# Moving the first expert's PSUM eviction from VectorE to ScalarE in a fused recurrent-attention and mixture-of-experts layer

## The reference

```
r  = sigmoid(xn @ Wr.T);  k = xn @ Wk.T;  v = xn @ Wv.T
scale  = exp(position * log(sigmoid(decay)))
state  = cumsum(k * v / max(scale, 1e-10), over tokens) * scale
s      = rmsnorm(r * state) @ Wo.T

scores = xn @ gate_w.T                        # 8 experts
onehot = one_hot(argmax(scores))
moe    = xn + sum over e of onehot[e] * (xn @ expert_w[e].T)
out    = x + s * silu(moe)
```

## Time and profile before

| | |
|---|---|
| time, median of 3 runs | 1269.22 us (1264.96 to 1271.9) |
| the profiled execution, its own time | 1270.49 us |
| its span on the slowest core (core 1) | 1268.9 us (other cores from 1261.4 us) |
| TensorE busy, matmuls | 910.5 us, 72% |
| VectorE busy | 691.3 us, 54% |
| ScalarE busy | 453.0 us, 36% |
| mean granted TensorE clock, core 1 | 0.911 of full speed |

### The profile page before, as it was taken

One profiled execution on the slowest core, in us unless ns is written; L12 is line 12 of the kernel. 1 busy time (PEld: TensorE's weight loads), 2 busy tenths in 40 slices (PEclk: granted clock), 3 DMA queues, 4 the chain that ended last, 5 costly groups with the idle time before them and its releaser, 6 DMA issues.

```text
span 1268.9 us, 17472 instructions; the slowest of 8 cores (1261.4 to 1268.9 us)
## 1 busy us (share of the span) xinstructions
PE 910.5 (72%) x5760; PEld 552.7 (44%) x5760; DVE 691.3 (54%) x1381; ACT 453.0 (36%) x929; POOL 95.4 (8%) x236
## 2 busy tenths in 40 slices
PE   1221236666566658899899899899899899799774
PEld 0111125455445544554454455455455355365231
DVE  4777755656665335454474473473573573563543
ACT  4444443333323254404604603703802802802102
POOL 0000001111111100000000000000000000000000
PEclk9999997777777779899899899899999999899887
DMA  3333335887876794544584584584674674574760
GB/s 102 106 110 115 117 129 111 201 206 198 201 178 163 202 269 164 199 169 163 191 249 161 201 262 149 197 263 156 207 251 160 228 259 159 186 239 145 233 211 34
DMA packets 39978, 229.81 MB, mean 181 GB/s; under 512 B 6096, under 2 KB 8144, under 8 KB 30672
## 3 DMA queue, kind: packets, MB, share of 16 engines
q0 software_dynamic: 19584, 167.78, 42.7%
q1 hardware_dynamic: 20304, 60.91, 14.8%
HBM read 220.28 MB, written 25.17 MB: 193 GB/s over the span
## 4 chain that ended last, share of the span: by engine, by line
PE 57%; DVE 23%; ACT 7%; issue 6%; DMA 5%; DVEq 1%; SPq 0%; ACTq 0%; POOL 0%; POOLq 0%
PE pb L605 25%; PE pb L501 24%; DVE qwb L271 5%; PE pb L659 4%; DMA ebuf<-escr 3%; DVE sC L267 3%; DVE sC L555 2%; PE pb L277 2%; DVE wvT L292 2%; DVE wkT L292 2%; ACT xn_fm L414 2%; DVE sD L539 2%; DVE sD L549 2%; PE pb L408 1%; ACT sA L348 1%
## 5 line engine op out<-in xcount | busy, mean ns | idle before, releaser
L605 PE MATMUL pb<-ebuf,xn_fm 128*128 128x512 bf16 x2048 | 469.2, 390 | 48.0 <-DVE moe L621 26.7
L605 PEld LDWEIGHTS pb<-ebuf,xn_fm 128*128 128x128 bf16 x2048 | 203.3, 100 | 303.8 <-issue 82.0
L621 DVE SCALAR_TENSOR_TENSOR moe<-pb,ohb,moe 128x512 bf16<-128x512 f32 x224 | 167.8, 749 | 74.4 <-PE pb L605 58.4
L277 PE MATMUL pb<-identb,qwb 128*128 128x128 bf16 x384 | 48.6, 306 | 212.2 <-DVE qwb L271 212.2
L501 PE MATMUL pb<-xn_fm,wkT 128*128 128x256 bf16 x1024 | 134.8, 300 | 7.0 <-ACT xn_fm L414 7.0
L277 PEld LDWEIGHTS pb<-identb,qwb 128*128 128x128 bf16 x384 | 37.1, 137 | 223.5 <-issue 223.5
L501 PEld LDWEIGHTS pb<-xn_fm,wkT 128*128 128x128 bf16 x1024 | 109.1, 107 | 32.6 <-issue 8.9
L501 PE MATMUL pb<-xn_fm,wvT 128*128 128x256 bf16 x1024 | 114.4, 273 | 2.7 <-DVE sC L523 2.7
L501 PEld LDWEIGHTS pb<-xn_fm,wvT 128*128 128x128 bf16 x1024 | 100.2, 98 | 16.0 <-issue 3.0
L583 POOL DMA_DIRECT2D ebuf<-escr x64 | 34.7, 543 | 725.0 <-PE pb L605 693.2
L257 ACT ACTIVATE sA<-stageQ 128x1024 f32<-128x1024 f32 x48 | 50.7, 1057 | 98.3 <-DVE sC L267 96.5
(11 more groups left out here) (101 smaller groups left out, 839.0 us busy)
## 6 DMA issues: line engine op xcount, KB each, us to landing
ebuf<-escr POOLq DMA_DIRECT2D x64, 2048.0 KB, 9.8
ebuf<-ewt POOLq DMA_DIRECT2D x64, 256.0 KB, 12.7
escr<-ebuf POOLq DMA_DIRECT2D x8, 2048.0 KB, 7.5
stageQ<-wk SPq DMA_DIRECT2D x16, 512.0 KB, 3.3
stageQ<-wv SPq DMA_DIRECT2D x16, 512.0 KB, 3.2
xb<-xpre SPq DMA_DIRECT2D x16, 512.0 KB, 8.4
xb<-xmain SPq DMA_DIRECT2D x16, 512.0 KB, 12.6
stageQ<-xmain SPq DMA_DIRECT2D x16, 512.0 KB, 10.4
```

Source lines behind the costliest of these rows:

```text
L277: return [e.matmul(bank[:, i2 * 128:(i2 + 1) * 128], qwbf[:, (4 * q + i2) * 128:(4 * q + i2 + 1) * 128], ident[:], start=True, stop=True) ...
L605: ins.append(e.matmul(bank[:, 0:512], xnf[:, kc * ST + j * 128: kc * ST + (j + 1) * 128], kbuf[:, kc * D + nh * 512: kc * D + nh * 512 + 512],
L621: e.scalar_tensor_tensor(dst, bank[:, 0:512], ohcol, src2, ALU.mult, ALU.add)],
```

## The change

A second copy of the one-hot matrix, `ohb2`, is made on VectorE right after `emit_gate` has produced `ohb`. The eviction of expert 0 then runs on ScalarE as an activation (identity, with the one-hot column from `ohb2` as its scale) instead of on VectorE as a `tensor_scalar`.

```diff
+        ohb2 = [sb(f"ohb2{i}", [128, 2 * 8]) for i in range(2)]
...
+            op("vector", lambda e, ohx=ohx, pp=pp: [
+                e.tensor_scalar(ohb2[pp][:], ohx[:], 1.0, None, ALU.mult)],
+               reads=[f"ohb{pp}"], writes=[f"ohb2{pp}"])
...
                         if ex == 0:
-                            op("vector", lambda e, dst=dst, bank=bank, ohcol=ohcol: [
-                                e.tensor_scalar(dst, bank[:, 0:512], ohcol, None, ALU.mult)],
-                                reads=[bk, f"ohb{pp}"], writes=["moe1"])
+                            ohcol2 = ohb2[pp][:, j * 8 + ex: j * 8 + ex + 1]
+                            op("scalar", lambda e, dst=dst, bank=bank, ohcol2=ohcol2: [
+                                e.activation(dst, bank[:, 0:512], AF.Identity,
+                                             scale=ohcol2)],
+                                reads=[bk, f"ohb2{pp}"], writes=["moe1"])
```

## The result

The changed kernel takes **1310.48 us** (median of 9 runs) against 1269.6 us (10 runs of the kernel before): a ratio of 1.032, 95% interval 1.031 to 1.034, 41 us slower. Forecast were 1301, an own range of 1296 to 1306, and a full range of 1290.5 to 1311. The profiled execution took 1309.25 us, its slowest core 1307.7 us (core 7; the others from 1296.9 us).

The account below looks back on a forecast made before the run. Bound: a chain without slack from expert 0's matmuls over VectorE and ScalarE to expert 3. 1270.49 + 30.9 (seven periods) + 0.8 (last step) = 1302.2 us profiled, 1301 median; range 1290.5 to 1311, own range 1296 to 1306.

Parts of the forecast that it names:

- both of its parts: Expert 0's evictions on ScalarE, 3.5 us per step, and the copy into `ohb2`, 1.2 us: together 4.71 us per step.
- dearer evictions: Expert 0's evictions on ScalarE at 0.75 us instead of 0.69, taken in by the range's upper end of 1311.
- the rival on the clock: TensorE falls to 1.2 GHz in expert 4 or at expert 3's end, 1.3 to 1.7 us per step: 1313; chance 0.10.
- The chain through `sB`: Eviction, table load and sigmoids in a row on ScalarE: `sB` starts 11.4 us after expert 0's start, 3.5 us later.
- The drain: Rival at ScalarE's table switch: up to a second load's time, 1.3 us, more per step: 1311; chance 0.02.
- only part 1 costs: Rival: the copy's wait costs TensorE nothing, only moving the evictions does, 3.5 us per step: 1294.5; chance 0.10.
- not slower: Rival: only expert 2 starts late, and the layer norm ends while it runs, so nothing is lost: 1269; chance 0.05.
- The wait ahead of expert 2: TensorE idles 5.4 us for VectorE's eviction instead of for the weights; expert 2, even at slow clock, stays hidden.
- The copy: VectorE's wait for `ohb` delays expert 3's evictions and so expert 4 on TensorE: 1.2 us of each step's 4.71.
- A constant period of 101.4 us: Sign in the profile after: every step from 0 to 6 takes 101.4 us, on each core.
- The sum was too small: Seven periods, 710.0 us against 679.06, add 30.9 us; step 7 adds 0.8: 1302.2 us profiled, 1301 median.
- Step 7: Last step, with no next one: only expert 1's evictions matter, +0.8 us, bounds 0 and 3.5.

Follow-up runs that it names:

- table_early: The changed kernel with a one-column sigmoid on ScalarE ahead of expert 0's evictions, so the table loads earlier: 1299.19 us, 1.024 of the kernel before.
- last_on_vector: The changed kernel with expert 0's fourth eviction back on VectorE and three left on ScalarE: 1291.08 us, 1.019 of the kernel before.
- copy_only: The changed kernel with expert 0's evictions back on VectorE; the copy into `ohb2` stays, unread: 1280.99 us, 1.010 of the kernel before.
- no_copy: The changed kernel without the copy; expert 0's evictions stay on ScalarE and read `ohb` itself: 1298.84 us, 1.024 of the kernel before.
- sig_first_no_copy: The changed kernel with the four sigmoids ahead of expert 0's evictions on ScalarE, and `ohb` read directly, no copy: 1249.41 us, 0.984 of the kernel before.

## Why the prediction was right, and what it mis-sized

The chain that it named is the one that the runs show, and both of its parts have their price. The size came out too small: 40.9 us for 31.8. 1310.48 lies outside the forecast's own range of 1296 to 1306 and only 0.5 us inside the full one, whose upper end had been set for dearer evictions and for the rival on the clock. Evictions were not dearer, and the clock gave only a small part of the excess, so that the full range still held it is partly luck.

- **The chain through `sB`**: right, 11.39 us measured for 11.4. The eviction (0.69), the table load at 1.30 with its seam and the sigmoids (2.07) stood as summed; table_early takes out the load (1.43 us earlier), last_on_vector the eviction and its place (1.73).
- **The drain**: the Trainium skill ("ScalarE: Activation LUTs", What ACT_TABLE_LOAD costs) has a drain on top of the load. The traces disagree, and this rival is out: by the seam in the changed kernel (697.77 to 699.08, 1.31 us) and by table_early.
- **The other rivals**: "only part 1 costs" is out by copy_only and no_copy, which differ from the kernel before and from the changed one by 10.3 and 10.8 us in the seven steps; "not slower" by the result.
- **The wait ahead of expert 2**: 5.65 us for a forecast of 5.4, and the slow clock in expert 2 (8.64 us) was hidden, as the step said; the transposes waited for `xn_tm` all the same.
- **The copy**: right in kind. Expert 4 at 43.00 us for 42.91. Its price alone is 12.3 us in the median and 10.3 in the seven steps, for 8.5 forecast (7 x 1.2): copy_only's mean period is 98.2 us where the floor is 97.7, and the mean period before was 96.7.
- **A constant period of 101.4 us**: steps 3 to 5 have 101.4 to 101.5 on every core, after 95.3 to 98.3 before. This was the strongest sign that the model was right. It was forecast for all of steps 0 to 6; steps 0 and 6 have up to 101.8, step 1 101.8 to 102.3, step 2 101.8 to 103.6.
- **The sum was too small**: seven steps grew by 36.0 us in the mean of the cores, for 30.9. Of the 5.1: 2.2, because I took the growth from the one core with the longest seven steps before (679.06, where the mean is 676.9); 1.7, four standing waits of 0.07 us in each of steps 1 to 6, for which the sum had no term, as it let `ybf` start right behind `sB`; about 2.6, slow clock and longer waits in single steps; less 1.4, the gate's chain from L389's end to `ohb`'s end being 13.08 us long, not 13.28.
- **The clock**: the rival was right in kind, but not in place or size. In step 2, expert 7 took 1.7 us more on six of eight cores (769.89 above). In step 1, experts 3 and 4 ran in one piece on the same six, with a granted clock of 0.64 in the first 8 us, so that expert 3 ended behind the copy's floor, some 0.5 us late:

```profile
621.58 16.82 PE L609 MATMUL pb<-ebuf,xn_fm 128*128 128x512 bf16 x64
```

In the mean of the cores, the slow stretches of both steps together are about 1.7 of the 2.6 us. The rest is waits longer by 0.35 us on all cores, such as 2.18 us in place of 1.83 ahead of expert 7 in step 2, and 0.78 in place of 0.43 ahead of L389 in step 1. What made them longer is open. The low clock did not reach into expert 4 in step 2 (7.07 us), nor in step 1 (granted clock 1.00 from 628.00 on).
- **Outside the seven steps**: over all executions the mean of the cores grew by 42.9 us (1260.6 to 1303.5), the median of the slowest core by 40.9. The seven steps of the two profiled executions have 36.0 of it, the part ahead of them 0.8. Some 6 us are not placed: the profiled execution of the kernel before was 4.2 us longer than its mean, that of the changed one 1.5 shorter. Step 7 was forecast at 0.8; the last steps of the two profiled executions differ by 0.4, less than their own scatter over the cores (99.6 to 108.0).
- **The slowest core**: core 7 of the profiled execution had a last step of 108.0 us where the mean is 103.4, with a wait of TensorE of 9.43 us for VectorE. VectorE itself waits there for a store of the output, since `s_sb` is written again. Core 7 of the changed kernel, then core 6 of the one before:

```profile
1261.50 1.23 DVE L709 TENSOR_TENSOR s_sb<-stageQ,sD 128x1024 f32<-128x1024 f32 x1 [9.58 <-DMA out<-s_sb]
```

```profile
1224.49 1.23 DVE L703 TENSOR_TENSOR s_sb<-stageQ,sD 128x1024 f32<-128x1024 f32 x1 [10.96 <-DMA out<-s_sb]
```

Every core has this wait, 6.1 to 11.0 us long before and 6.1 to 9.6 in the changed kernel. So the change does not make it longer; it is one of the things that decide which core is the slowest.

## What to carry to other kernels

An operation moved to an idle engine lands in that engine's queue, and what stands behind it there is delayed until its input comes: ScalarE was busy for only 36% of the span, and still the move cost 30 us there, for the four sigmoids that used to run ahead of their need. Before moving work, list what is queued behind the new place and who waits for that, and put the moved work behind whatever is ready earlier. A helper copy on another engine's queue is a wait too: it cost 1% here though nothing needed it.

## What the runs showed that I had not expected

- A wait for a semaphore value reached long before costs about 0.07 us on VectorE: the gap ahead of `ybf` is 0.38 us with five waits (one on VectorE itself, four on TensorE), 0.17 us with two, and 0.10 with one (before, 688.65 to 688.75). Moving an operation away from an engine can bring such waits out, since its own wait had covered them.
- The releaser named in the trace for those 0.38 us was wrong, because its end fell into the gap; in table_early, with the same length, the trace names `sB`.
- ScalarE can read as its scale a column that ScalarE itself wrote some 60 us earlier; the copy by another engine was not needed (no_copy, sig_first_no_copy).
- A shift of 0.2 us ahead of expert 2 went together with the loss of a slow stretch of 1.7 us in expert 7 of step 2, some 60 us later, on all six cores that had it, in one profiled execution of each kernel. Such slow stretches come and go with small shifts, and no forecast of mine can place them.
